# Six orders of words for TensorE's moving operand in the second pass of a float32 FFN

## The reference, cut to what matters

```python
W = weights[condition]                                  # (32, 64, 64)
y = einsum('bct,bcd->bdt', x, W)
h = gelu(einsum('bsd,df->bsf', y, inter_w) + inter_b, approximate=True)   # 1024 -> 4096
out = x + einsum('bsf,fd->bsd', h, output_w) + output_b                   # 4096 -> 1024
```

## Time and profile before

| | |
|---|---|
| times of the runs without profile | 1215.87 us and 3175.93 us (2 runs; median 2195.9 us) |
| time of the profiled execution | 1217.55 us |
| its span, first to last instruction | 1215.4 us |
| TensorE busy in matmuls, share of the span | 1210.0 us, 100% |
| VectorE (DVE), ScalarE (ACT), GpSimd (POOL) | 73%, 46%, 23% |
| granted TensorE clock, mean | 1.00 of full speed |

### The profile page before, as it was taken

How to read it: one execution, slowest core, us unless ns; L and a number is a source line. 1 busy time by engine, 2 the same in 40 slices (tenths; PEclk the granted TensorE clock), 3 DMA queues, 4 the chain that set the end, 5 groups by cost and what they waited for, 6 DMA issues and landing times.

```text
span 1215.4 us, 15226 instructions
## 1 busy us (share of the span) xinstructions
PE 1210.0 (100%) x5468; PEld 1007.2 (83%) x5468; DVE 885.0 (73%) x1132; ACT 560.5 (46%) x961; POOL 273.8 (23%) x188
## 2 busy tenths in 40 slices
PE   9999999999999999999999999999999999999999
PEld 9888888888888888888888888888888888888887
DVE  5997797878656556665548678577788676788886
ACT  4845555555444444444445444444444444444443
POOL 4352233222306334423301121101100101101000
PEclk9999999999999999999999999999999999999999
DMA  9597668866998544665399999756863749956553
GB/s 342 156 303 249 220 239 297 290 233 217 400 397 243 135 123 132 184 189 132 95 336 283 347 286 271 214 191 161 191 176 112 188 127 243 288 187 181 190 150 110
DMA packets 119868, 267.62 MB, mean 220 GB/s; under 512 B 9938, under 2 KB 19442, under 8 KB 118386
## 3 DMA queue, kind: packets, MB, share of 16 engines
q1 hardware_dynamic: 105248, 232.81, 54.5%
q0 software_dynamic: 13824, 33.56, 16.3%
q10 hardware_dynamic: 722, 0.28, 0.1%
HBM read 174.34 MB, written 92.27 MB: 219 GB/s over the span
## 4 chain that ended last, share of the span: by engine, by line
PE 98%; DMA 2%; DVE 0%; issue 0%; ACT 0%; ACTq 0%
PE ps L703 50%; PE ps L719 44%; DMA h_raw<-p_mem 2%; PE ps L651 1%; PE ps L666 1%; PE ps L738 0%; PE ps L746 0%; DVE lhs L1080 0%; ACT lhs L896 0%; DVE rhs L1083 0%; DVE out L1244 0%; DVE ones L1180 0%; ACTq L893 0%
## 5 line engine op out<-in xcount | busy, mean ns | idle before, releaser
L703 PE MATMUL ps<-y,lhs 128*128 128x512 f32 x2688 | 610.9, 389 | 1.1 <-issue 1.1
L703 PEld LDWEIGHTS ps<-y,lhs 128*128 128x128 f32 x2688 | 504.2, 188 | 105.5 <-issue 1.2
L719 PE MATMUL ps<-rhs,lhs 128*128 128x512 f32 x2472 | 560.8, 389 | 0.4 <-DVE rhs L1083 0.4
L719 PEld LDWEIGHTS ps<-rhs,lhs 128*128 128x128 f32 x2472 | 463.9, 188 | 97.1 <-DVE lhs L1080 0.8
L896 ACT ACTIVATE lhs<-h_raw 128x512 fp32r<-128x512 f32 x208 | 131.5, 632 | 323.6 <-PE ps L719 316.1
L1080 DVE TENSOR_TENSOR lhs<-h_raw,lhs 128x512 fp32r<-128x512 f32 x208 | 144.1, 693 | 125.5 <-ACT lhs L896 125.4
L983 DVE TENSOR_TENSOR lhs<-w_raw,lhs 128x512 fp32r<-128x512 f32 x128 | 110.3, 863 | 128.9 <-ACT lhs L802 128.9
L802 ACT ACTIVATE lhs<-w_raw 128x512 fp32r<-128x512 f32 x128 | 81.0, 633 | 174.5 <-PE ps L703 171.5
L1083 DVE TENSOR_TENSOR rhs<-w_buf,rhs 128x512 fp32r<-128x512 f32 x208 | 142.3, 684 | 0.0
L901 ACT ACTIVATE rhs<-w_buf 128x512 fp32r<-128x512 f32 x208 | 128.0, 615 | 0.0
L983 DVE TENSOR_TENSOR lhs<-s_w,lhs 128x512 fp32r<-128x512 f32 x96 | 75.1, 786 | 57.7 <-ACT lhs L802 57.3
(11 more groups left out here) (53 smaller groups left out, 551.4 us busy)
## 6 DMA issues: line engine op xcount, KB each, us to landing
h_raw<-p_mem SPq DMA_DIRECT2D x80, 512.0 KB, 4.9
w_raw<-in_L_ffn_inter_w_dram SPq DMA_DIRECT2D x31, 1024.0 KB, 8.0
p_mem<-part SPq DMA_DIRECT2D x96, 256.0 KB, 6.1
w_buf<-in_L_ffn_output_w_dram SPq DMA_DIRECT2D x12, 2048.0 KB, 15.2
q_mem<-part SPq DMA_DIRECT2D x64, 256.0 KB, 5.9
h_raw<-q_mem POOLq DMA_DIRECT2D x32, 512.0 KB, 6.7
y_mem<-y_out SPq DMA_DIRECT2D x28, 512.0 KB, 3.4
y<-y_mem SPq DMA_DIRECT2D x7, 2048.0 KB, 13.9
```

The lines of the kernel that those rows point to most:

```text
L703: last = nc.tensor.matmul(ps[:, bank, :], w[:, k, :], y[i][:, part, k, :], start=(i in FRESH and k == 0 and u == 0), stop=(k == KH - 1 and ...
L719: last = nc.tensor.matmul(ps[:, bank2(t, tb), :], lhs[s % RING][:, a, blk(tb)], rhs[r][:, w, :], start=(t in FRESH2 and q == 0 and u == 0) ...
```

## The change

The second pass's y pieces are stored in another order of words for six of the seven products. Per product i and block k, the 1024 words of a partition (z = 0 the high part, z = 1 the low part, and 512 tokens t of each) lie as follows. Steps are in words of 4 bytes, and the order in which TensorE takes the tokens is the same as before:

- i = 0: high part, then low part, 512 words each, as before.
- i = 1: high and low words alternate. A matmul reads 512 words with a step of 2.
- i = 2: tokens b*2 + a lie at a*256 + b. A matmul reads word 0, 256, 1, 257, 2, 258 and so on.
- i = 3: a matmul reads 256 words with a step of 2, then the 256 words between them.
- i = 4: tokens b*16 + a lie at a*32 + b. A matmul reads 16 words with a step of 32 (128 bytes), goes back to one word past the start, and reads again 16 words with a step of 32, and so on.
- i = 5: runs of 16 adjacent words, in turn from two places 256 words apart.
- i = 6: runs of 16 adjacent words (64 bytes), one every 32 words; the low part fills the gaps.

`y1_high` and `y1_low` write the pieces by these patterns (their source is still read in 512 adjacent words, and DVE's second input, the high part, is read by the pattern). `y_mem` is laid out so that an item is one run of 1024 words per partition, before it was two of 512 words; the loads move 16 KB per partition in one run, as before. `y[i]` as a tile keeps its place; in the second pass it is addressed as 4 blocks of 1024 words. The first pass reads y in the plain order. No instruction, DMA or wait is added, removed or moved; the diff's core:

```diff
-    y_mem = nc.dram_tensor("y_mem", [PRODUCTS, P, 2, KH, BANK], F32, kind="Internal").ap()
+    y_mem = nc.dram_tensor("y_mem", [PRODUCTS, P, KH, 2 * BANK], F32, kind="Internal").ap()
-        y1_out = [at(f"y1_out{i}", 192 + 4 * i, [2, BANK], F32R) for i in range(2)]
+        y1_out = [at(f"y1_out{i}", 192 + 4 * i, [2 * BANK], F32R) for i in range(2)]
+        def layout(i, flat):
+            if i == 0:
+                return flat.rearrange("p (z t) -> p z t", z=2)
+            if i == 1:
+                return flat.rearrange("p (t z) -> p z t", z=2)
+            if i == 2:
+                return flat.rearrange("p (z a b) -> p z b a", z=2, a=2)
+            if i == 3:
+                return flat.rearrange("p (z b a) -> p z a b", z=2, a=2)
+            if i == 4:
+                return flat.rearrange("p (z a b) -> p z b a", z=2, a=16)
+            if i == 5:
+                return flat.rearrange("p (z a c b) -> p z c a b", z=2, a=2, b=16)
+            return flat.rearrange("p (c z b) -> p z c b", z=2, b=16)
+        def as_in(i, tokens):
+            if i == 2:
+                return tokens.rearrange("p (b a) -> p b a", a=2)
+            if i == 3:
+                return tokens.rearrange("p (a b) -> p a b", a=2)
+            if i in (4, 6):
+                return tokens.rearrange("p (b a) -> p b a", a=16)
+            if i == 5:
+                return tokens.rearrange("p (c a b) -> p c a b", a=2, b=16)
+            return tokens
+        def y_part(n, i, part, k):
+            if n < NG:
+                return y[i][:, part, k, :]
+            return layout(i, y[i][:].rearrange("p a k t -> p (a k t)")[:, 2 * BANK * k:2 * BANK * (k + 1)])[:, part]
...
-                sp.dma_start(y_mem[i][:, :, kb, :], y1_out[item % 2][:].bitcast(F32)).then_inc(y1_kept[item % 2], 16)
+                sp.dma_start(y_mem[i][:, kb, :], y1_out[item % 2][:].bitcast(F32)).then_inc(y1_kept[item % 2], 16)
...
-                        last = nc.tensor.matmul(ps[:, bank, :], w[:, k, :], y[i][:, part, k, :],
+                        last = nc.tensor.matmul(ps[:, bank, :], w[:, k, :], y_part(n, i, part, k),
...
-                nc.scalar.activation(y1_out[item % 2][:, 0, :], y1_in[:, (0, 0, 0, 3, 1, 2, 2)[i], :], ACT.Copy).then_inc(y1_hi, 1)
+                nc.scalar.activation(layout(i, y1_out[item % 2][:])[:, 0], as_in(i, y1_in[:, (0, 0, 0, 3, 1, 2, 2)[i], :]), ACT.Copy).then_inc(y1_hi, 1)
...
-                nc.vector.tensor_tensor(o[:, 1, :], y1_in[:, (0, 0, 0, 3, 1, 2, 2)[i], :], o[:, 0, :].bitcast(F32),
+                nc.vector.tensor_tensor(layout(i, o)[:, 1], as_in(i, y1_in[:, (0, 0, 0, 3, 1, 2, 2)[i], :]), layout(i, o)[:, 0].bitcast(F32),
                                         ALU.subtract).then_inc(y1_split, 1)
```

More of the change, by code:

```diff
@@ L380, in load_y @@
                 sp.wait_ge(step_done, step1(NG - 1, 2 * i + 2))
-                sp.dma_start(y[i][:].bitcast(F32), y_mem[i]).then_inc(y_in[i], 16)
+                sp.dma_start(y[i][:].rearrange("p a k t -> p (a k t)").bitcast(F32), y_mem[i].rearrange("p k z -> p (k z)")).then_inc(y_in[i], 16)
             def load_h(n):
@@ L1175, in y1_low @@
                 dve.wait_ge(y1_hi, item + 1)
-                o = y1_out[item % 2]
-                nc.vector.tensor_tensor(o[:, 1, :], y1_in[:, (0, 0, 0, 3, 1, 2, 2)[i], :], o[:, 0, :].bitcast(F32),
+                o = y1_out[item % 2][:]
+                nc.vector.tensor_tensor(layout(i, o)[:, 1], as_in(i, y1_in[:, (0, 0, 0, 3, 1, 2, 2)[i], :]), layout(i, o)[:, 0].bitcast(F32),
                                         ALU.subtract).then_inc(y1_split, 1)
```

## The result

The changed kernel takes 1345.8 us (median of 2 runs, 1345.41 and 1346.22), against 1215.87 us for the run before that agrees with the profile: ratio 1.107, interval 1.105 to 1.108. It is slower by 130 us. The run of 3175.93 us before was never seen again: 27 later runs of the kernel before, beside the experiments, took 1215.2 to 1218.3 us.

What follows compares the result with a forecast made beforehand. TensorE's matmul pace, set by how fast words enter the array, was taken as the bound. Gain 0, staging 0 and reading +84.5 us on 1217.55 gave 1302 us profiled, 1300 us without profile; range over the cases 1213 to 1395 us.

Steps and rivals of the forecast that it cites:

- Part 1: Possible gain over the whole kernel: nothing, as no instruction or wait goes; lower end -1 us.
- the 13 ns above 213.3 ns: Matmul pitch beyond one column per period of 2.4 GHz; taken as the price of changing weights, which stays.
- Part 2: Staging in the first pass, 24 items written by a pattern: cost 0, or 16 us were the cover gone.
- The bound of a doubling: Upper bound for patterned staging writes in the first pass: 15 us on ScalarE and 16 us on VectorE.
- Part 3: TensorE's moving operand in the second pass: products 2 and 4 pay +220 ns a matmul, the others 0; +84.5 us.
- The upper bound: Slowest price of a pattern per second-pass matmul, from the warm-up's pace: 920 ns for 512 columns, +693 ns.
- C: Rival: TensorE needs four words per access; step 2 at half pace, products 2 and 4 slowest; 1566 us; chance 0.08.
- the odd cases: All outcomes beside the forecast and the named rivals; chance 0.02.
- A: Rival: TensorE reads any word at full pace, so patterns cost nothing; 1216 us; chance 0.28.
- B: Rival: an access brings two adjacent words, so products 1 to 4 run at half pace; +169 us, 1385 us; chance 0.15.
- D: Rival: a reader keeping two places open reads product 2 freely, only product 4 pays; +42 us, 1258 us; chance 0.09.
- E: Rival: staging loses its cover in the first pass, adding up to 16 us to whichever case holds; no separate chance.

Runs made afterwards that it cites:

- the bench: Kernels without the whole computation: TensorE alone, or VectorE and ScalarE alone, one access pattern per line; TensorE's adjacent words took 226.7 ns per matmul.
- all2: Against the kernel before, all seven products of the second pass stored and read by the pattern of product 2: 1206.3 us, ratio 0.992.
- stage_only: The changed kernel's six staged orders, but TensorE reads all pieces as adjacent words (output wrong): 1216.2 us, ratio 1.000 to the kernel before.

## Why the prediction was right or wrong

- **What bounds the kernel: right.** TensorE's pace was the only thing that mattered; 129.9 of 130 us are in the pitch, and no new wait appeared.
- **Part 1, nothing can be gained: wrong.** I took the 13 ns above 213.3 ns for a change of weights, because both matrix products show them. All rows before were of adjacent words, so they couldn't tell a price of the weights from a price of the reading. In the bench two places take 10.9 of the 13 ns away with the same weights, and all2 shows it in the kernel. The forecast for this change hardly suffered, as the 10 ns of product 2 are 1.9 us.
- **Part 2, the staging costs nothing: right**, shown by stage_only. The bound of a doubling was nearly met by products 2 and 4 (1143 to 1175 ns on ScalarE), and the cover held.
- **Part 3, the sorting of the patterns: wrong, and the step that failed.** "Two words taken one after another lie close together" is not what counts. It gave 0 for products 1 and 3, which measured +226 and +224 ns, and +220 ns for product 2, which measured -10. Product 4 was right (+208 for +220). Products 5 and 6 pay 14 ns for 32 changes of place, where I had 0. What fits the measured pitches is the distance between every second word: 4 words for step 2, 1 word for two places. That the sum came as near as 84.5 for 129.9 us is luck: one product too many was taken for slow and two too few.
- **The size of the slow pace: right by luck.** 446 ns were forecast, and products 1, 3 and 4 took 435 to 452. But the 446 were scaled from the mixing's 111.6 ns for 128 columns, and that row reads adjacent words, so it holds no price of a step. In the bench (type `F32R`; the mixing is plain float32) 128 adjacent words take 110.3 ns and 256 take 119.4: a short matmul is that slow per column without any step. The upper bound, the warm-up's 230 ns, is of adjacent words too. Besides, the trace's record of the clock begins at 6.86 us, so that the 1.00 of the window from 1.22 to 6.28 us is no measured clock. The distance of two matmuls falls from 213 to 112 ns at about that time, so the row was likely taken at the lower clock, which is not shown.
- **The sums** come out otherwise. The one slip is the share that the range leaves out: C and the odd cases are 0.08 + 0.02, 1 in 10 and not 1 in 8.
- **The rule of the Trainium skill** ("Advanced Engine Details and Errata", "SBUF Cachelines": at least two hits on a line of 16 bytes) holds for ScalarE and VectorE with plain steps: 655 and 686 ns for step 2, 1107 and 1056 for step 4. It doesn't hold for their reads from two places (735 and 698 ns). For TensorE, read for the whole sequence as I did, it is wrong in both directions (453 ns for step 2, 215.8 for two places). Counted for each of two streams it fits the plain steps and the two places, and not the pairs, the four or the eight places.
- **The rivals.** A (no price) is refuted by products 1, 3 and 4. B had 1, 3 and 4 right and failed on 2. C had 1 and 3 right, but its deeper loss didn't come: the slowest pattern of the bench took 488 ns, not 920. D had product 2 free and 4 slow, with the idea of two places that stay open, and missed 1 and 3. Taken together, B for products 1, 3 and 4 and D for product 2, they would have given 3 x 192 x 0.220 = 127 us. E cost nothing.

## What to carry to other kernels

When a pace is a few per cent off the round number and every row shows the same access pattern, the rest may belong to the pattern; one bench with a pattern per line settles it in one run. Here it turned a change that lost 130 us into one that gains 49: of the orders tried, a moving operand of type `F32R` with 512 columns is read fastest when every second word is the neighbour of the one two before. A step of 2 halves TensorE's pace. In SBUF it costs ScalarE and VectorE little alone and some 150 to 200 ns for 512 words beside a TensorE that reads in turn, and in a read of PSUM it costs nothing. So put the step there.

## What was not expected of the hardware

- Adjacent words aren't the fastest order for TensorE: 226.7 ns for 512 columns, against 215.8 ns in turn from two places at 4 to 8192 words' distance.
- A plain step of 2 words costs TensorE about as much as a step of 32 (453 and 433 ns), and more than four places (283 ns) or sixteen (433 ns); only eight places (488 ns) and streams that step by 8 words (460 and 462 ns) were slower.
- ScalarE and VectorE read from two places at 735 and 698 ns, but write to two places at 1096 and 1051 ns.
- The order in which TensorE reads changes what a read costs others: ScalarE's copy with step 2 takes 662 ns beside adjacent reading and 872 beside reading in turn. A copy of adjacent words keeps its 615 to 618 ns.
- After 3.1 us without a matmul the granted clock fell to its lower level (eight matmuls at 427 ns, some 3.4 us) in a kernel whose matmuls had followed one another without a gap since 367 us.
